# Output product of a state space layer computed from high and low parts on one Trainium2 core

## The reference, cut to what matters

```
y, _final = ssd(x * dt[..., None], A * dt, Bh, Ch, CHUNK)
y = y + x * D[None, None, :, None]
y = y.reshape(b, s, D_SSM)
y = y * silu(z)
var = jnp.mean(jnp.square(y), axis=-1, keepdims=True)
y = y * jax.lax.rsqrt(var + EPS) * norm_scale
return y @ W_out
```

## Time and profile before

| what | value |
| --- | --- |
| median of 3 runs | 1043.91 us (1041.44 to 1048.77) |
| profiled execution, its own time | 1038.18 us |
| its span, first to last instruction | 1036.5 us |
| mean granted PE clock | 0.995 of full speed |
| busy: PE, DVE, ACT, POOL | 984.7, 733.9, 576.4, 290.9 us |
| share of the chain that ended last: PE, DVE, ACT, POOL | 77%, 13%, 6%, 1% |

### The profile page before, as it was taken

The page is one execution under the profiler, slowest core; times in us unless marked ns, Lnnn a source line. Parts: engine busy times, 40 slices in busy tenths (PEclk is TensorE's granted clock), DMA queues, the critical chain, the costliest instruction groups (busy, mean ns, idle before and its releaser), DMA issues.

```text
span 1036.5 us, 17973 instructions
## 1 busy us (share of the span) xinstructions
PE 984.7 (95%) x6609; PEld 785.7 (76%) x6609; DVE 733.9 (71%) x1449; ACT 576.4 (56%) x1257; POOL 290.9 (28%) x210
## 2 busy tenths in 40 slices
PE   7989999999999799999999999999999999989996
PEld 5545689999997567588777878878888787968753
DVE  3666456555553679888887987978878777658566
ACT  3445344444442321287767767777677677946634
POOL 6910054444442300000002222422405422113412
PEclk9999999999999999999999999999999999999999
DMA  8560066665531333122003464524413203065100
GB/s 272 132 246 1 3 226 242 231 212 212 212 122 57 104 93 89 48 77 60 21 24 78 82 111 65 106 41 90 87 37 84 81 5 98 1 232 239 66 1 21
DMA packets 65981, 109.16 MB, mean 105 GB/s; under 512 B 19409, under 2 KB 44145, under 8 KB 64754
## 3 DMA queue, kind: packets, MB, share of 16 engines
q1 hardware_dynamic: 65906, 108.17, 35.2%
HBM read 103.24 MB, written 4.91 MB: 104 GB/s over the span
## 4 chain that ended last, share of the span: by engine, by line
PE 77%; DVE 13%; ACT 6%; issue 2%; DMA 1%; POOL 1%; SPq 0%; DVEq 0%; POOLq 0%; ACTq 0%
PE PS L1680 16%; PE PS L1553 12%; PE PS L1669 10%; PE PS L1657 8%; PE PS L1572 6%; PE PS L1642 4%; PE PS L1772 3%; DVE scores L1175 2%; PE PS L1694 2%; ACT scores L840 1%; PE PS L1453 1%; PE PS L1815 1%; PE PS L1612 1%; PE PS L1621 1%; DVE pL L1228 1%
## 5 line engine op out<-in xcount | busy, mean ns | idle before, releaser
L1228 DVE TENSOR_TENSOR pL<-PS,pH 128x512 fp32r<-128x512 f32 x256 | 175.9, 687 | 63.3 <-ACT pH L864 62.9
L864 ACT ACTIVATE pH<-PS 128x512 fp32r<-128x512 f32 x256 | 151.9, 596 | 100.0 <-PE PS L1669 100.0
L840 ACT ACTIVATE scores<-scores,nmX 128x512 f32<-128x512 f32 x256 | 185.3, 724 | 18.5 <-DVE nmX L1179 18.5
L1175 DVE TENSOR_SCALAR_CACHE_REDUCE scores<-PS 128x512 f32<-128x512 f32 x256 | 172.7, 683 | 14.7 <-PE PS L1657 14.3
L1680 PE MATMUL PS<-pH,kvH 128*128 128x256 f32 x512 | 164.5, 321 | 6.6 <-ACT xnT L849 6.6
L1669 PE MATMUL PS<-ident,scores 128*128 128x128 f32 x1024 | 157.0, 276 | 1.1 <-DVE pL L1228 0.9
L1680 PE MATMUL PS<-pL,kvH 128*128 128x256 f32 x512 | 143.9, 281 | 0.0
L1680 PE MATMUL PS<-pH,kvL 128*128 128x256 f32 x512 | 143.6, 281 | 0.0
L1669 PEld LDWEIGHTS PS<-ident,scores 128*128 128x128 f32 x1024 | 117.4, 140 | 31.7 <-issue 16.4
L1680 PEld LDWEIGHTS PS<-pH,kvH 128*128 128x128 f32 x512 | 96.7, 189 | 10.8 <-issue 10.6
L1680 PEld LDWEIGHTS PS<-pL,kvH 128*128 128x128 f32 x512 | 97.2, 190 | 0.0
(11 more groups left out here) (310 smaller groups left out, 2247.4 us busy)
## 6 DMA issues: line engine op xcount, KB each, us to landing
rawG<-in_wg SPq DMA_DIRECT2D x16, 768.0 KB, 5.6
rawU<-in_wu SPq DMA_DIRECT2D x16, 768.0 KB, 7.0
rawD<-in_wd SPq DMA_DIRECT2D x16, 768.0 KB, 6.2
wrow<-in_w SPq DMA_DIRECT2D x11, 512.0 KB, 4.1
xn<-in_w1t SPq DMA_DIRECT2D x11, 512.0 KB
wturned<-turned SPq DMA_DIRECT2D x4, 1056.0 KB, 13.3
wb<-w_rows SPq DMA_DIRECT2D x32, 128.0 KB, 3.3
wqX<-in_wqX SPq DMA_DIRECT2D x16, 256.0 KB, 2.6
```

Source lines behind the costliest of these rows:

```text
L840: act.activation(at, at, ACT.Exp, bias=nmX[:, p % 2, h, q:q + 1], accum_out=csum[:, p % 2, NT * h + q, c:c + 1]).then_inc(exp_done, 1)
L864: act.activation(pH[:, i % 4], PS[:, 2 + i % 2, :].rearrange("p (k t) -> p k t", t=T), ACT.Copy).then_inc(pH_ready, 1)
L1175: dve.tensor_scalar(sp_[:, h, q, c * CH:(c + 1) * CH], PS[:, 4 * q + h, :], 1.0, None, ALU.mult, ALU.max, accum_out=cmax[:, h, q, c:c + 1] ...
L1228: dve.tensor_tensor(pL[:, i % 4], PS[:, 2 + i % 2, :].rearrange("p (k t) -> p k t", t=T), pH[:, i % 4].bitcast(F32), ALU.subtract).then_in ...
```

## The change

`wout` is split once into a high part `woutH` and a low part `woutL`, both F32R, by POOL: `high_out` copies half of the slices (2048 columns) into an F32R room, and `low_out` subtracts that from `wout`, in place. The first half's high part has a room of its own (`woutH0`), the second half's lies over the room of `xp`, which is free after the last tap. POOL does the first copy after slices 0 to 3 of `weighted`, the first subtract after cv4, then slices 4 and 5, then the second copy and subtract, then slices 6 and 7.

`yn` becomes `ynH`, F32R, by the same ACT instruction, and DVE makes `ynL` from `yz`, the scale and `ynH` after waiting for `ynH`. PE's `project` does three F32R products in place of one of F32: ynH with woutH, ynL with woutH, ynH with woutL. It waits for `ynL` in place of `yn`, and for the two halves of the split in place of the DMA.

```diff
+        woutL = sb("woutL", [P, IT, D], F32R, early)
+        early.close()
         wout = A("wout", [P, IT, D])
...
+        woutH1 = sb("woutH1", [P, IT // 2, D], F32R, early)
+        early.close()
         xp = A("xp", [P, CT, CONV - 1 + T]); cv = A("cv", [P, CT, T]); act_ = A("act_", [P, CT, T])
...
-        yn = A("yn", [P, 2, T]); y2 = A("y2", [P, 2, T]); y2s = A("y2s", [P, T])
+        woutH0 = A("woutH0", [P, IT // 2, D], F32R); ynH, ynL = (A(n, [P, 2, T], F32R) for n in ("ynH", "ynL")); y2 = A("y2", [P, 2, T]); y2s = A("y2s", [P, T])
...
+            def high_out(half, room):
+                step(pool.tensor_copy(room[:], wout[:, half * IT // 2:(half + 1) * IT // 2]))
+
+            def low_out(half, room):
+                part = slice(half * IT // 2, (half + 1) * IT // 2)
+                pool.tensor_tensor(woutL[:, part], wout[:, part], room[:].bitcast(F32), ALU.subtract).then_inc(ssm_consts, 1)
+
             for m in range(IT // 2):
                 weighted(m)
+            pool.wait_ge(wout_in, 16)
+            high_out(0, woutH0)
             pool.wait_ge(ssm_dve.sem, ssm_dve.at("cv4", 2))
-            for m in range(IT // 2, IT):
+            low_out(0, woutH0)
+            for m in range(IT // 2, UA):
+                weighted(m)
+            high_out(1, woutH1)
+            low_out(1, woutH1)
+            for m in range(UA, IT):
                 weighted(m)
...
-                    act.activation(yn[:, m % 2], yz[:, m % 2], ACT.Copy, scale=ns[:, m:m + 1]).then_inc(yn_ready, 1)
+                    act.activation(ynH[:, m % 2], yz[:, m % 2], ACT.Copy, scale=ns[:, m:m + 1]).then_inc(yn_ready, 1)
...
                 dve.tensor_tensor(yz[:, m % 2], yt[:, m % 2], zs[:, m], ALU.mult).then_inc(yz_ready, 1)
+                dve.wait_ge(yn_ready, m + 1)
+                wait(dve, o_done, m - 1)
+                dve.scalar_tensor_tensor(ynL[:, m % 2], yz[:, m % 2], ns[:, m:m + 1], ynH[:, m % 2].bitcast(F32), ALU.mult, ALU.subtract).then_inc(ssm_dve.sem, 1)
...
             def project(m, t):
-                return pe.matmul(PS[:, t, :], yn[:, m % 2, t * P:(t + 1) * P], wout[:, m, :], start=(m == 0), stop=(m == IT - 1))
+                high = woutH0[:, m] if m < IT // 2 else woutH1[:, m - IT // 2]
+                for c, (v, w) in enumerate(((ynH, high), (ynL, high), (ynH, woutL[:, m]))):
+                    mm = pe.matmul(PS[:, t, :], v[:, m % 2, t * P:(t + 1) * P], w, start=(m == 0 and c == 0), stop=(m == IT - 1 and c == 2))
+                return mm
...
-            pe.wait_ge(wout_in, 16)
+            pe.wait_ge(ssm_consts, 6)
             for m in range(IT):
                 ssm_out(m)
+                if m - 1 == IT // 2:
+                    pe.wait_ge(ssm_consts, 7)
                 if m:
-                    pe.wait_ge(yn_ready, m)
+                    pe.wait_ge(ssm_dve.sem, ssm_dve.at("ynL", m))
```

More of the change, by code:

```diff
@@ L215, in perceiver @@
         arena = ExitStack()
+        early = ExitStack()
+        woutL = sb("woutL", [P, IT, D], F32R, early)
+        early.close()
         wout = A("wout", [P, IT, D])
@@ L290, in perceiver @@
         ssm_act = Marks(sem("ssm_act"), dte=2, tap0=2, tap1=2, silu0=2, tap2=2, silu1=2, tap3=2, silu2=2, tap4=2, silu3=2, silu4=2)
-        ssm_dve = Marks(sem("ssm_dve"), dta=1, a=1, cv0=2, cv1=2, cv2=2, gm=1, cv3=2, cv4=2, xdt=NT)
+        ssm_dve = Marks(sem("ssm_dve"), dta=1, a=1, cv0=2, cv1=2, cv2=2, gm=1, cv3=2, cv4=2, xdt=NT, ynL=IT)
         late_pe = Marks(sem("late_pe"), ss=1, yo=NT, xqT0=1, gu0=2, xqT1=1, gu1=6, hqT0=2, hqT1=3)
@@ L1839, in _ @@
             mm.then_inc(late_pe.sem, 1)
-            pe.wait_ge(yn_ready, IT)
+            pe.wait_ge(ssm_dve.sem, ssm_dve.at("ynL", IT))
             for t in range(NT):
```

## The result

The changed kernel takes 1048.11 us (median of 20 runs, 1043.71 to 1052.60), the kernel before 1041.71 (20 runs): a ratio of 1.0057, 95% interval 1.0043 to 1.0072, or 5.9 us (4.5 to 7.5) by that ratio. Forecast were 6.8 us more, on the earlier median 1050.7. It is within 1%, as the likeliest case had it; with 20 runs of each kernel the interval is 0.3% wide, so the difference is told from none, which the prediction held possible only from 1% on.

What follows compares the result with a forecast made beforehand. PE looked like the bound at 3.64 us a slot, with a DVE and ACT loop of 3.38 right behind. Stall 6.2 plus clock 0.6 gave +6.8 us: 1045.0 on the profiled scale, 1050.7 on the median's; range 1045.5 to 1057.

Steps and rivals of the forecast that it cites:

- the likeliest case: Whole kernel: within 1% of no change, given 0.80; the forecast itself had 0.70, from +3 to +10 us.
- The stall: State space loop: POOL's late split blocks DVE and delays the copy of the first square; 6.2 us added.
- the clock: PE half idle from 976 to 990 us drops to 1.2 GHz: nothing to 1.7 us, 0.6 taken.
- ynL and POOL's additions of squares: Late slices of the loop: the two meet, 0.1 us a slice, +0.3 us.
- The upper bound of 3.8: POOL's 128x2048 copy: at most 3.8 us, by the two-operand pass over 1024 columns; 1.9 taken.
- A copy blocks too: POOL copies block DVE's two-SBUF-operand instructions as subtracts do; were copies free, the sum would be 0.4 us less.
- The first copy: From 950 to 952 us it blocks DVE's taps for 1.9 us, hidden by DVE's later wait of 3.18.
- the rival in which it stays low: PE at 1.2 GHz through slices 4 to 7, slots of 6.2 us: +18 us, 1062; chance 0.05.
- The mis-sized term: PE's loop slot: six fp32r rows at 1.38 us replace 1.91, so 3.64 falls to 3.11 us.
- the covered rival: POOL's work stays under its 5.9 us of slack: 0.3 to 4.2 us faster, 1039.7 to 1043.6; chance 0.12.
- POOL dearer: POOL's copies take 4.6 us, as a subtract, lengthening the same stall: about +12 us, 1056; chance 0.10.
- fp32r rows: PE's output product: rival that these rows cost 0.48 us each, slot 4.6: +11.6 us, 1055.5; chance 0.03.

Runs made afterwards that it cites:

- the first experiment: Changed kernel without GpSimd's first subtract, second copy and second subtract, first half's high part as weight in all products: ratio to kernel before 0.9997.

## Why the prediction was right

*The stall.* Right in place, cause and size. Counted from the transposes, mask 2 was to end at 15.40 us and ended at 15.08, the copy of the first square was to end at 21.04 and ended at 20.59, and mask 4 was to start at 22.24. It started at 23.01, and at 21.92 with PE kept awake. So at mask 4 the stall is 5.9 us where 6.2 were summed, and the clock 1.1 where 0.6 were taken; at the end of the stage they are 5.8 and 0.75. The errors have opposite signs and cancel, which is luck: 6.96 at mask 4, 6.57 at the end of the stage, 6.8 forecast. One part of the stall was not there at all: ynL and POOL's additions of squares were to cost 0.3 us in the late slices, but ynL takes 0.48 there, the same each time, and the period is 3.39.

*POOL's instructions.* The subtract, extrapolated to 4.59 us, took 4.55 and 4.61. The copy, extrapolated from 128 and 256 columns to 1.9, took 1.89 where DVE stood idle (the subtracts on VectorE) and 2.08 beside DVE's work. The upper bound of 3.8 was not needed.

*A copy blocks too.* Taken from the subtract without a row for it; ynL's 1.45 us, ending 0.28 behind the copy, now is that row. The section "SBUF: two separate sides" of the page SBUF — State Buffer of the Trainium skill had said so of any GpSimd operation that reads SBUF, and the trace agrees for copies now (1.45 us in place of 0.48).

*What costs nothing.* The first copy: 26.81 us from the first tap to the transposes with and without it, with DVE's idle time 2.25 in place of the 3.18 of the earlier trace rows; so it held up the taps by 0.93 us where 1.9 were taken, and the idle time hid it as forecast. ynL and the six rows: nothing, by the first experiment.

*The clock.* Right in kind: PE gapped and fell to the lower level for 6 to 7 us, where the one stretch of before lasted 3.4. It came back under steady work, so the rival in which it stays low fell. I had put its price on PE's rows; it was paid on ACT, as 0.98 us of waiting for one log decay.

*The mis-sized term.* The slot was to fall from 3.64 to 3.11 us; it fell to 3.30 to 3.33. The chain's 1.91 us for the old product and 0.46 for two fp32r rows are shares of a path, and six such rows are not three times two. The stretch from the start of the product to the next `onesR` row holds the product and one pair of decay rows, so by these terms it was to be 1.91 + 0.46 = 2.37 us before and 1.38 + 0.46 = 1.84 after. It was 985.72 - 983.44 = 2.28 before and 1002.59 - 1000.63 = 1.96 after, 0.32 saved and not 0.53; the first of the six rows takes 0.34 to the next, not 0.23. The `onesR` rows, before and after:

```profile
985.72 0.40 PE L1796 MATMUL PS<-ua,onesR 128*128 128x256 f32 x2
```
```profile
1002.59 0.40 PE L1819 MATMUL PS<-ua,onesR 128*128 128x256 f32 x2
```

The term did not enter the sum, as PE's saving was counted as hidden, but it carries the covered rival's best end: 8 x 0.32 = 2.6 us, not 4.2. The first experiment brings that rival's case about, and gave 0.40 us of stage, its small end.

*The rivals.* Covered work needed a subtract of 2.0 us; it took 4.6. POOL dearer needed copies of 4.6; they took 2.1. fp32r rows cost 0.23 to 0.24 (0.34 for the first of a slice), not 0.48. The clock came back.

## What to carry to other kernels

A side job on GpSimd has two prices that its duration does not show: VectorE's instructions with two SBUF operands wait for the whole of each of its instructions (here up to 4.34 us in one mask), and whatever GpSimd does for the loop stands behind it. Both have to go before anything is won back: cut long instructions or place them where VectorE waits for someone else, and put what the loop wants ahead of them. And a saving on the busiest engine is to be read against the floor of the loop right behind it: here 3.38 against 3.64.

## What the runs showed of the hardware that was not expected

The same 128x2048 pass to fp32r took 1.23 us on VectorE, 1.89 on ScalarE and 1.89 on GpSimd (2.08 to 2.69 where VectorE worked beside it), and the subtract 2.29 on VectorE against 4.55 to 4.61 on GpSimd (up to 5.12 where it had to wait): a side job that seemed free on the idle engine was about half as long on the busy one, and fitted a wait of its own there. And moving a GpSimd instruction earlier can cost as much as it wins, since it meets other VectorE work (1.20 won, 1.16 lost).
